# SP's transfers in the loop of a fused audio tower: the copy of the keys between the halves of the weights' broadcast

## The reference, cut to what matters

```
h = relu(conv over 8 taps, 128 -> 64 channels, scaled by filt) # 248 windows
h = h + attention(layernorm(h))     # one head, D = 64, over the 248 windows of a sequence
h = h + moe(layernorm(h))           # 8 experts 64 -> 128 -> 64, the two best of a gate's logits
```

## Time and profile before

| | us |
|---|---|
| median of 3 runs (lowest, highest) | 303.11 (302.2, 304.63) |
| the profiled execution | 303.27 |
| its span on the core | 301.5 |
| PE busy | 282.9 (94%) |
| DVE, ACT, POOL busy | 242.5 (80%), 238.8 (79%), 103.7 (34%) |
| transfers: mean rate over the span | 91 GB/s |

### The profile page before, as it was taken

How to read it: one execution, slowest core, us unless ns; L and a number is a source line. 1 busy time by engine, 2 the same in 40 slices (tenths; PEclk the granted TensorE clock), 3 DMA queues, 4 the chain that set the end, 5 groups by cost and what they waited for, 6 DMA issues and landing times.

```text
span 301.5 us, 6202 instructions
## 1 busy us (share of the span) xinstructions
PE 282.9 (94%) x1737; PEld 202.9 (67%) x1737; DVE 242.5 (80%) x889; ACT 238.8 (79%) x549; POOL 103.7 (34%) x99
## 2 busy tenths in 40 slices
PE   7778989999999899999999999999999999998992
PEld 7546557776776667676777768677766776655571
DVE  2376678989897888988897979899898889895765
ACT  3256788898898789898998988888988779876661
POOL 2112123342526143441525171534424151505060
PEclk9997999999999999999999999999999999999999
DMA  6312206080623517080715335170803324153301
GB/s 185 107 24 79 72 3 169 4 205 18 154 71 80 144 37 188 4 220 2 180 47 136 86 96 129 55 170 5 212 11 90 83 87 120 45 128 83 73 19 34
DMA packets 12785, 27.58 MB, mean 91 GB/s; under 512 B 3152, under 2 KB 5456, under 8 KB 12752
## 3 DMA queue, kind: packets, MB, share of 16 engines
q1 hardware_dynamic: 12464, 26.91, 34.9%
q10 hardware_dynamic: 288, 0.28, 0.3%
HBM read 20.85 MB, written 2.27 MB: 77 GB/s over the span
## 4 chain that ended last, share of the span: by engine, by line
PE 66%; DMA 16%; DVE 9%; issue 4%; ACT 4%; SPq 1%; ACTq 0%; DVEq 0%
PE bank_y L1355 16%; DMA kk<-kk 14%; PE bank_a L1271 10%; PE bank_h L1344 8%; PE bank_h L1345 7%; PE bank_s L1288 5%; PE bank_s L1393 4%; PE bank_s L1299 4%; DVE kk L963 2%; PE bank_b L1364 1%; PE bank_b L1404 1%; DMA x<-xt 1%; PE bank_s L1360 1%; PE bank_s L1364 1%; PE bank_b L1360 1%
## 5 line engine op out<-in xcount | busy, mean ns | idle before, releaser
L461 ACT ACTIVATE hid<-bank_h,col 128x496 f32<-128x496 f32 x128 | 84.0, 672 | 13.1 <-PE bank_h L1345 10.6
L370 POOL TENSOR_TENSOR p<-p,rmask 124x496 f32<-124x496 f32 x32 | 32.5, 1017 | 99.3 <-DVE rmask L845 99.2
L1355 PE MATMUL bank_y<-hid,w_sb 128*64 128x248 f32 x512 | 64.3, 380 | 0.7 <-DVE acc L809 0.7
L1344 PE MATMUL bank_h<-xs,w_hi 128*128 128x496 f32 x128 | 58.2, 454 | 0.2 <-DVE xs L255 0.2
L809 DVE SCALAR_TENSOR_TENSOR acc<-bank_y,col,cb 128x248 f32<-128x248 f32 x128 | 53.7, 469 | 5.5 <-PE bank_y L1355 2.1
L1355 PEld LDWEIGHTS bank_y<-hid,w_sb 128*64 128x64 f32 x512 | 32.9, 136 | 25.4 <-issue 12.2
L1345 PE MATMUL bank_h<-xs,w_lo 128*128 128x496 f32 x128 | 49.5, 386 | 0.0
L264 POOL TENSOR_TENSOR total<-acc 128x496 f32<-128x496 f32 x16 | 20.1, 1255 | 44.2 <-DVE acc L809 43.8
L452 ACT ACTIVATE p<-bank_s,nmax 124x248 f32<-124x248 f32 x64 | 29.3, 466 | 1.3 <-DVE nmax L834 0.8
L384 POOL TENSOR_TENSOR x_lo<-x,x_hi 128x512 fp32r<-128x512 f32 x16 | 20.4, 1275 | 27.1 <-ACT x_hi L520 27.1
L1344 PEld LDWEIGHTS bank_h<-xs,w_hi 128*128 128x128 f32 x128 | 24.1, 189 | 7.2 <-issue 3.9
(11 more groups left out here) (116 smaller groups left out, 555.2 us busy)
## 6 DMA issues: line engine op xcount, KB each, us to landing
cb<-weights SPq DMA_DIRECT2D x60, 248.0 KB, 4.2
kk<-kk SPq DMA_DIRECT2D x16, 248.0 KB, 4.3
x<-xt SPq DMA_DIRECT2D x15, 256.0 KB, 5.1
out<-h SPq DMA_DIRECT2D x16, 124.0 KB, 3.5
w_sb<-w SPq DMA_DIRECT2D x3, 256.0 KB, 4.0
wtok_sb<-wtok SPq DMA_DIRECT2D x1, 256.0 KB, 2.6
x<-xt ACTq DMA_DIRECT2D x1, 256.0 KB, 4.1
weights<-ct_sb SPq DMA_DIRECT2D x15, 15.5 KB, 1.4
```

The lines of the kernel that those rows point to most:

```text
L370: pool.tensor_tensor(p_sb[b][0:HALF, :, :], p_sb[b][0:HALF, :, :], rmask[0:HALF, b, :].unsqueeze(2).to_broadcast([HALF, 2, WIN]), ALU.mult ...
L461: act.activation(hid[2 * (p % 2) + s][:, :], bank_h[s][:, 0:TOK], ACT.Relu, bias=col[:, C_B1 + e:C_B1 + e + 1]).then_inc(hid_ready[s], 1)
L1344: pe.matmul(bank_h[e % 2][:, 0:TOK], w1_hi[:, e, :], xs[m % 2][:, :], start=True, stop=False)
L1355: last = pe.matmul(bank_y[p % 2][b * D:b * D + D, s * WIN:(s + 1) * WIN], w2_sb[:, 2 * p + s, :], hid[2 * (p % 2) + s][:, b * WIN:(b + 1) ...
```

## The change

In each of the ten iterations of the loop, SP's copy of the keys is put between the two halves of the weights' broadcast; the load of x then follows the second half. In `fill` the copy of the second group's keys changes places with the load of group 5. Nothing else differs; all other engines have the same instructions in the same order.

```diff
@@ fill
                 copy_keys(0)
                 load(3)
                 load(4)
+                copy_keys(1)
                 load(5)
-                copy_keys(1)
                 store_weights(0)
                 spread(0, 0)
                 copy_keys(2)
@@ iteration
                 d, n, m = t, t - 2, t - 3
                 store_weights(n)
                 spread(n, 0)
+                copy_keys(d)
                 spread(n, 1)
                 load(t + 3)
-                copy_keys(d)
                 store(m)
```

## The result

| | before | changed |
|---|---|---|
| median of 16 runs (lowest, highest) | 303.08 us (300.86, 306.67) | 300.85 us (299.97, 303.9) |
| ratio, 95% interval | | 0.993 [0.9902, 0.9958] |
| the profiled execution | 303.27 us | 300.56 us |
| its span | 301.5 us | 298.7 us |

The change makes the kernel faster by 0.7%, between 0.4 and 1.0%: some 2.2 us where 3.0 were forecast. In this ratio and the later ones, executions more than 1.5% above the fastest of their kernel are left out.

A forecast was written before the change was run, and what follows sets the result against it. PE, 94% busy, waits 6.5 us before the scores for the key copy, queued behind other transfers; less 3.5 us that stay, 3.0 us gained: 303.27 becomes 300.3, median 300.2; range 299.4 to 301.4, 8 in 10 298.9 to 302.9.

The forecast's parts named there:

- (a): Loop's copy of the keys: issued as before, landing in 2.9 us (bounds 2.9 and 4.2) against a median of 4.7.
- (b): PE's scores (L1288): the logits' read (L863) leaves 0.35 us of wait per iteration, whatever the copy does.
- The sum: Waits before the scores: 6.5 us now, less 3.5 us that stay, gives 3.0 us gained.
- (c): Broadcast's second half, read by DVE's L809: lands later, cost 0, at least 1.9 us to spare.
- (d): Load of x, read by `high_inputs` (L520): issued later, cost 0, cover 6.2 us.
- (e): SP's queue behind the copy (second half, x, output store, next weights' store): cost 0, 3 us of cover.
- (f): Second copy in `fill`, ahead of one load of x: taken as 0, bounds 0 and 0.65 us.
- Full relief: Rival at the scores: the logits' wait moves forward too, 4.3 us gained, 299.0 us; chance 0.15.
- No dependence on the order: Rival: the copy's landing does not depend on the order, or freed time is lost elsewhere; 303.2 us; chance 0.16.
- The slower rival: DVE's L809: second half late; 1 us in each of ten iterations would cost 7 us, 310.3; chance 0.04.

The follow-up runs named there:

- e9: Kernel before with loop order half, half, copy, load, and half, half, load, copy in the last iteration; 299.1 us, 0.9887 of before.
- e4: Kernel before with only the change in `fill` (second copy ahead of the load of group 5), loop as before; 302.78 us, 1.0018 of before.
- e8: Kernel before, SP's order kept, with only the logits moved ahead of the masks on DVE; 302.88 us, 0.9979 of before.
- e5: On top of e1, DVE reads the logits and splits the tokens ahead of the masks in the loop; 298.24 us, 0.9862 of before.
- e6: On top of e1, the broadcast's second half goes out last in the loop, behind load and output store; 299.76 us, 0.9935 of before.
- e2: Kernel before with loop order half, half, copy, load, so the load of x goes behind the copy; 299.59 us, 0.9918 of before.
- e1: Changed kernel, but in the loop's last iteration (t = 12) the load of x goes ahead of the copy; 299.39 us, 0.9913 of before.
- e7: On top of e1, the broadcast's second half goes out last and is held until PE has done the first scores; 305.17 us, 1.0107 of before.
- c3: e5 run once more; 297.77 us, 0.983 of before.
- c1: The changed kernel run once more; 300.6 us, 0.9944 of before.
- c2: e1 run once more, beside c1; 299.22 us, 0.9901 of before.
- e3: Kernel before with order half, load of x, copy, half in all ten loop iterations; 300.22 us, 0.994 of before.

## Why the prediction was right, and where not

(a) Right. The loop copies were put at 2.9 us, bounds 2.9 and 4.2; they took 2.9 to 3.2. The instances of the order that `fill` and `drain` already held gave the value. The issue did not move, as said. `e9` and the unchanged loops of `e4` and `e8` show that it is the order.

(b) Right in place and size. Forecast: 0.35 us stay in each iteration, with the loads 0.12 us behind the logits. Eight of ten show 0.35 to 0.37 us of the loader's idle time; the exceptions are 0.65 us at t = 5 (so "0.35 us remains in each iteration, whatever the copy does" is not quite so) and 0.10 us for the last, which stands in `drain`'s order. `e5` and `e8` show that it is the logits. The sum's 3.0 us came as 2.58 + 0.33 = 2.9 in the pair of profiles. Set against the loop of `e4` (149.48 us) instead, the nine iterations gained 2.1 us.

(c) Right: DVE has no wait for a broadcast before L809 in the changed kernel's loop except for the late first half at t = 5 (0.41 us, put down to "issue"):

```profile
DVE acc L809 <- issue: 0.6, 2, 0.4
```

Even in `e6` the last piece landed 1.5 us before its reader.

(d) Wrong for the last iteration. It took the next reader of the load, L520 at 161.90, as that of every iteration: "Cost 0, cover 6.2 us". The last load has another reader's time, since `drain` has `high_inputs(15)` two instructions behind `high_tokens_2(11)`, 5.5 us after the load's issue, and not 15 us after it. Before, L520 began at 219.00 with x landing at about 218.95 (issued at 213.45, 5.5 us to landing): there was no cover at all (in `e4` and `e8`, with the old order, ACT waited 0.7 and 0.4 us there). The load now goes out 2.8 us later against the projection, which cost 1.6 to 1.9 us of ACT's wait, and 0.9 to 1.3 us against a kernel whose last load is early. The rows for it were in the trace of before, at one place out of ten.

Whether (d) is what made the forecast too large is open. The medians fell short of the sum by 0.8 us. The last load's 0.9 to 1.3 us and the 0.86 us near the end of `drain` (last section) are together more than that, and the old order loses part of the first as well. `e2`, which also issues its last load behind the copy, stands level with `e1` beside which it ran (299.6 and 299.4 us). The 3.0 us also lie at the edge of the interval of the measured gain (1.3 to 3.0 us), so the shortfall itself is small against the scatter.

(e), (f) Right: nothing queued on SP became late in the loop, and `fill` is worth nothing (`e4`).

The rivals. Full relief did not come by this change, and came when the logits were moved, at 298.2 and 297.8 us with the last load repaired; the forecast had 299.0. No dependence on the order is refuted, by the copies' times and by the waits that are gone. The slower rival did not occur; its estimate of 1 us per us late was about right in kind, with 0.63 us lost per iteration in `e7` for a piece that landed 0.7 to 1.2 us behind its reader's ordinary time.

By the Trainium skill's two-part price for a transfer ("DMA: Bandwidth & Descriptors", the two cost components) the change would be worth 0. The changed order gained, so the queue of transfers is real in this kernel. The measured 3.0 us of a copy with little ahead of it is not far from the 2.6 us estimated by that price. Rule and kernel part at the time that each further transfer takes, 1.05 us here and 0.58 by the estimate.

## What to carry to other kernels

If an engine waits for a transfer whose issue can't come earlier, look at what the transfer finds ahead of it: even one large transfer that nobody needs soon, issued just before, delays it (by 0.7 to 0.9 us here, where such transfers land 1.05 us apart). Before moving that transfer back, look up its reader at every place of the program, the first and last iterations apart, because there the order around it is another. And ask for the second wait at the same instruction: it sets how much of the first can be had, and is the next thing to remove.

## What the runs showed that I had not expected

The weights' store of 15.5 KB lands in 1.4 us, but in the loop's iterations t = 5 and t = 12 it took 2.2 to 2.6 us in every profile except one (`e7`: 1.7 at t = 5), and in some kernels in `drain` too. In the changed kernel, the stores of t = 5 (issued at 89.18 us) and of the iteration ahead of it:

```profile
weights<-ct_sb SPq DMA_DIRECT2D x1, 15.5 KB, 2.3
...
weights<-ct_sb SPq DMA_DIRECT2D x1, 15.5 KB, 1.4
```

The first half then comes late to L809; outside `e7`, DVE waits 0.3 to 1.3 us for it at t = 5. That iteration is then 16.8 to 17.7 us long with the logits behind the masks; with them ahead on top of the new order, in `e5` and `c3`, it is 16.5 and 16.3.

Near the end of `drain`, the copy of group 14's keys took 4.4 to 4.5 us in the changed kernel and in `e1`, `e5` and `e6`, and again in `c1`, `c2` and `c3`, but 2.9 to 3.0 us in before, `e3`, `e4`, `e7`, `e8` and `e9`, at one and the same order of SP's transfers there. It goes with a stretch from group 14's projection to group 15's of 16.4 us for 15.55. SP's second half behind it took longer to issue too; the changed kernel and then before:

```profile
245.26 0.48 SPq L309 DMA_DIRECT2D kk<-kk  x1
245.78 2.45 SPq L298 DMA_DIRECT2D cb<-weights  x2
```

```profile
248.86 0.48 SPq L309 DMA_DIRECT2D kk<-kk  x1
249.38 1.23 SPq L298 DMA_DIRECT2D cb<-weights  x2
```

The traces hold one thing that goes with both. The program's own instructions are loaded by transfers too, which the profile lists as queues of the kind "instruction". In the 14 profiles there are 210 weights' stores. All 39 that took 1.7 to 2.6 us had such a load under way within 1.4 us of their issue. Of the 171 that took 1.4 us one had, and it ended 0.03 us into the store. So it is with the copy of group 14's keys: each of the seven at 4.4 to 4.5 us, and the one of 4.8 in `e2`, had a load of instructions beginning 1.1 to 1.9 us after its issue, and none of the six at 2.9 to 3.0 us had one. The changed kernel from 245.2 to 250 us:

```profile
q8 instruction: 1, 0.02, 2.0%
```

A load at other distances from a copy went with ordinary times: in the changed kernel one began 0.74 us after the copy at 128.18, which took 3.2 us. No run moved these loads, so that they are the cause is not shown; but it would explain why a change of SP's order in the loop is followed by a loss in `drain`, where the order is the same: the loads fall at another distance from the transfers. Some 0.85 us are lost in every profile of the changed kernel and of its repaired forms `e1`, `c2`, `e5`, `c3` and `e6`, so this is not the chance of one execution.

The mask instruction L970 on 124x4 elements takes 0.65 us while POOL's addition (L264) runs beside it and 0.17 us where it does not. In each of the 14 profiles its long instances are those beside that addition. That a small instruction can take four times its time and carry a wait of PE with it was visible before, and I had read only its end.
